# The parts of the turned maxima made on GpSimd instead of VectorE, in a fused attention and mixture-of-experts kernel

## The reference

```python
x = x + 0.5 * _L0_ffn_ref(_layernorm(x), ...)      # 8 experts, the 2 best by a router
x = x + _L0_attn_ref(_layernorm(x), ...)           # 16 heads of 16, causal, 1024 x 1024 scores a head
x = x + 0.5 * _L0_ffn_ref(_layernorm(x), ...)

# in _L0_attn_ref
scores = jnp.einsum('bhqd,bhkd->bhqk', q, k) * (1.0 / np.sqrt(HD))
scores = scores * causal - (1.0 - causal) * NEG
attn = jax.nn.softmax(scores, axis=-1)
out = jnp.einsum('bhqk,bhkd->bhqd', attn, v)
```

## Time and profile before

| | us |
|---|---|
| median of 3 runs | 996.08 (994.55 to 997.16) |
| the profiled execution | 996.42 |
| its span, first to last instruction | 994.7 |
| attention at a steady pace, groups 1 to 13 | 357.06 to 698.25 |
| one slot there | 26.24 |

### The profile page before, as it was taken

The page is one execution under the profiler, slowest core; times in us unless marked ns, Lnnn a source line. Parts: engine busy times, 40 slices in busy tenths (PEclk is TensorE's granted clock), DMA queues, the critical chain, the costliest instruction groups (busy, mean ns, idle before and its releaser), DMA issues.

```text
span 994.7 us, 17662 instructions
## 1 busy us (share of the span) xinstructions
PE 955.4 (96%) x5602; PEld 567.4 (57%) x5602; DVE 830.3 (83%) x2445; ACT 511.0 (51%) x1053; POOL 264.3 (27%) x288
## 2 busy tenths in 40 slices
PE   6899998999998899999999999999998999999998
PEld 4678886777776233333333333333344777777776
DVE  6677777688686899999999999999768788888775
ACT  4235423424315677777777777777775333232310
POOL 1012204202205222222221221222343553434210
PEclk9999999999999899999999999999999999999999
DMA  6201121101023433223222322233320111110001
GB/s 225 90 1 64 51 77 65 37 28 64 34 63 97 128 77 77 78 73 75 61 76 61 72 66 66 72 78 77 92 61 13 43 65 64 64 56 21 8 22 42
DMA packets 55109, 64.32 MB, mean 65 GB/s; under 512 B 13824, under 2 KB 37360, under 8 KB 55024
## 3 DMA queue, kind: packets, MB, share of 16 engines
q1 hardware_dynamic: 54432, 62.47, 22.1%
q10 hardware_dynamic: 592, 0.80, 0.2%
HBM read 41.30 MB, written 21.23 MB: 63 GB/s over the span
## 4 chain that ended last, share of the span: by engine, by line
PE 85%; DVE 7%; issue 3%; ACT 2%; POOL 2%; DMA 1%; DVEq 0%; SPq 0%; ACTq 0%; POOLq 0%
PE bank L362 39%; PE bank L1611 14%; PE bank L1435 13%; PE bank L1593 13%; PE bank L857 2%; PE bank L354 2%; POOL a_part L496 1%; DVE bank L1462 1%; ACT b_probs L1570 1%; DMA v_all<-L_ffn_w_experts 1%; DVE a_acc L1081 1%; PE bank L803 1%; DVE c_acc L1081 1%; POOL b_ks L1408 1%; DVE a_st L317 1%
## 5 line engine op out<-in xcount | busy, mean ns | idle before, releaser
L1570 ACT ACTIVATE b_probs<-bank 128x512 f32<-128x512 f32 (+1 forms) x608 | 302.9, 587 | 114.8 <-PE bank L1593 114.4
L1462 DVE CUSTOM_DVE_ANT_0 bank<-bank,b_below 128x384 f32<-128x384 f32 (+3 forms) x512 | 235.2, 515 | 10.8 <-PE bank L1435 9.3
L1435 PE MATMUL bank<-b_ks,b_qs 96*128 96x512 bf16 (+3 forms) x768 | 222.8, 331 | 10.1 <-DVE b_neg L1462 4.1
L1593 PE MATMUL bank<-b_qs,b_ks 99*128 99x512 bf16 (+3 forms) x768 | 214.9, 331 | 4.5 <-ACT b_probs L1570 4.3
L362 PE MATMUL bank<-we,a_xt 128*128 128x512 f32 x768 | 194.2, 405 | 0.9 <-DVE a_acc L1081 0.9
L362 PE MATMUL bank<-we,c_xt 128*128 128x512 f32 x768 | 186.2, 398 | 0.9 <-DVE c_acc L1081 0.8
L1541 POOL TENSOR_SCALAR_AFFINE_SELECT b_probs<-b_probs 128x512 f32<-128x512 f32 x128 | 83.9, 656 | 323.9 <-ACT b_probs L1570 323.9
L1466 DVE TENSOR_REDUCE b_neg<-bank 128x1 f32<-128x512 f32 x256 | 161.2, 679 | 2.7 <-PE bank L1435 1.2
L362 PEld LDWEIGHTS bank<-we,c_xt 128*128 128x128 f32 x768 | 142.3, 188 | 33.5 <-DVE c_acc L1081 1.9
L362 PEld LDWEIGHTS bank<-we,a_xt 128*128 128x128 f32 x768 | 142.4, 191 | 28.9 <-DVE a_acc L1081 1.5
L1611 PE MATMUL bank<-b_probs,b_vs 128*32 128x512 f32 (+3 forms) x1536 | 156.6, 502 | 0.9 <-POOL b_probs L1541 0.9
(11 more groups left out here) (136 smaller groups left out, 891.1 us busy)
## 6 DMA issues: line engine op xcount, KB each, us to landing
b_qs<-q_parts SPq DMA_DIRECT2D x96, 128.0 KB, 3.0
b_ks<-k_parts SPq DMA_DIRECT2D x96, 128.0 KB, 3.0
q_parts<-a_part SPq DMA_DIRECT2D x16, 384.0 KB, 2.6
k_parts<-a_part SPq DMA_DIRECT2D x16, 384.0 KB, 2.7
att_num<-b_oev SPq DMA_DIRECT2D x64, 64.0 KB, 2.2
c_num<-att_num SPq DMA_DIRECT2D x8, 512.0 KB
c_rec<-att_rec SPq DMA_DIRECT2D x16, 256.0 KB
out<-xs SPq DMA_DIRECT2D x7, 512.0 KB, 3.3
```

Source lines behind the costliest of these rows:

```text
L1435: last = nc.tensor.matmul(ms[bank][:, a * width:(a + 1) * width], qs[g.u][0:ROWS, c, i * P:(i + 1) * P], ks[g.u][0:ROWS, c, lo:lo + width] ...
L1462: last = dve.tensor_tensor_reduce(part, part, below[:, CH - width:CH], -1.0, 3.0e38, ALU.add, ALU.min, dst[:, a, :])
L1570: act.activation(probs[b % 4][:, heads[0]:heads[0] + hp, 0:width], es[exp_bank(g, unit)][:, 0:hp * width].rearrange("p (h w) -> p h w", w= ...
L1593: last = nc.tensor.matmul(es[exp_bank(g, unit)][:, a * width:(a + 1) * width], ks[g.u][:, c, j * P:(j + 1) * P], qs[g.u][:, c, first_q:fir ...
```

## The change

VectorE keeps the copy out of PSUM (GpSimd's part works on the copy in SBUF). The four instructions that split the copy go, for groups 1 to 15, into GpSimd's queue, between its select of block 8 and its select of block 9 of the slot before. They wait for that select (`kept`), for the copy (`mread`) and, from the second use of a buffer on, for its earlier placing (`mplaced`); after them GpSimd waits for the last of them. Group 0's parts stay on VectorE. VectorE's copy now waits for the parts of the group before.

```diff
+    def maxima_parts(engine, g, position):
+
+        t, r, m = turned, turned_rest, mparts[g.u]
+        engine.wait_ge(mread, at(position + 1))
+        if g.turn:
+            engine.wait_ge(mplaced[g.u], at(16 * 3 * g.turn))
+        engine.tensor_copy(m[:, 0, :], t[:]).then_inc(mpart, 1)
+        engine.wait_ge(mpart, at(5 * g.n + 1))
+        engine.tensor_tensor(r[:], t[:], m[:, 0, :], ALU.subtract).then_inc(mpart, 1)
+        engine.wait_ge(mpart, at(5 * g.n + 2))
+        engine.tensor_copy(m[:, 1, :], r[:]).then_inc(mpart, 1)
+        engine.wait_ge(mpart, at(5 * g.n + 3))
+        engine.tensor_tensor(m[:, 2, :], r[:], m[:, 1, :], ALU.subtract).then_inc(mpart, 2)
+
     def max_read(dve, entry, position, bank):
         g, n = entry
         dve.wait_ge(mscore, at(position + 1))
         if n is None:
-            t, r, m = turned, turned_rest, mparts[g.u]
-            dve.tensor_copy(t[:], ms[bank][0:GH * KT, 0:P]).then_inc(mread, 1)
-            dve.wait_ge(mread, at(position + 1))
-            if not (isinstance(g.turn, int) and g.turn == 0):
-                dve.wait_ge(mplaced[g.u], at(16 * 3 * g.turn))
-            dve.tensor_copy(m[:, 0, :], t[:]).then_inc(mpart, 1)
-            dve.wait_ge(mpart, at(5 * g.n + 1))
-            dve.tensor_tensor(r[:], t[:], m[:, 0, :], ALU.subtract).then_inc(mpart, 1)
-            dve.wait_ge(mpart, at(5 * g.n + 2))
-            dve.tensor_copy(m[:, 1, :], r[:]).then_inc(mpart, 1)
-            dve.wait_ge(mpart, at(5 * g.n + 3))
-            dve.tensor_tensor(m[:, 2, :], r[:], m[:, 1, :], ALU.subtract).then_inc(mpart, 2)
+            dve.wait_ge(mpart, at(5 * g.n))
+            dve.tensor_copy(turned[:], ms[bank][0:GH * KT, 0:P]).then_inc(mread, 1)
+            if g.n == 0:
+                maxima_parts(dve, g, position)
             return
...
                     pool.affine_select(out=part, in_=part, compare_op=ALU.is_ge, fill=0.0, base=0,
                                        pattern=[[0, GH], [1, P]], channel_multiplier=-1).then_inc(kept, 1)
+                if b == 8 and exists(g + 1):
+                    pool.wait_ge(kept, at(len(sel_blocks) * g.n + sel_blocks.index(b) + 1))
+                    turn = [n for n, (entry, _, _) in enumerate(placed(g)) if entry[1] is None][0]
+                    maxima_parts(pool, g + 1, placed(g)[turn][1])
+                    pool.wait_ge(mpart, at(5 * (g.n + 1) + 5))
                 if b == 2 and exists(g + 1):
```

## The result

The changed kernel takes **1003.84 us** in the median of 4 runs (1003.48 to 1010.09), the kernel before 995.93 on the same chip: a ratio of 1.0096 [1.0074, 1.0118]. The change makes the kernel slower. 1003.6 us was forecast, and the way it was forecast, a wait in every steady slot for the placed parts, by which the slot grows 0.41 us, is what the trace shows.

A forecast was written before the change was run, and what follows sets the result against it. The prediction took TensorE to set the steady pace, with VectorE a close second. Its terms 5.3 + 0.6 + 0.4 + 1.2 = 7.5 us gave 1003.6 us; the forecast's own bounds were 999 to 1012, the stated range 996 to 1011.

The forecast's parts named there:

- step 1: VectorE loses four instructions in each of 15 groups, freed 1.15 us a slot; TensorE's rate hides it, counted as 0.
- step 2: The parts start behind select 8, which ends at 483.80, no longer behind the copy at 481.0.
- step 3: The four instructions take longer on GpSimd: 1.73 us in sum, ends 1.53 and 2.26.
- X: Time of GpSimd's chain from select 8's end to the last part: 1.73 us forecast; TensorE's wait begins at 1.32.
- step 4: At the next group's first exponential matmul TensorE waits 0.41 us for the placing, in 13 steady slots: 5.3 us.
- step 5: Slot 0 is tighter: its matmul comes at 357.68 against 357.06, 0.6 us.
- step 6: In slot 14 the chain runs beside VectorE's product c_att and is slowed: about 0.4 us, between 0 and 1.
- step 7: Single late issues or landings of placings are no longer hidden: some three events, 1.2 us, from 0 to 1.6.
- step 8: Select 9 with its products and the later loads, queued behind the parts and placings, cost 0.
- the cover holds: Rival: X is under 1.32, parts land before TensorE wants them; 994.7 to 996.5, say 995.8; chance 0.14.
- VectorE was the bound: Rival: TensorE only follows VectorE, so each of 15 groups gives 1.15 us; 17 us, 979; chance 0.05.
- mutual blocking: Rival: GpSimd and VectorE block each other in every slot, TensorE waits 1.51 a slot; 23 us, 1019; chance 0.07.

The follow-up runs named there:

- e1: The changed kernel with GpSimd's chain of four instructions moved ahead of select 8 in slots 0 to 13; 995.18 us, ratio 0.9997.
- e3: The changed kernel with SyncE placing each part as soon as it is there, not all three behind the last; 995.09 us, ratio 0.9997.
- e5: The kernel before with one more VectorE copy of 32 x 128 numbers in every slot; 998.26 us, ratio 1.0039.
- e2: The changed kernel with the first two of the four instructions back on VectorE, the last two on GpSimd behind select 8; 1005.32 us, ratio 1.0099.
- e4: The changed kernel with two more casts of the turned maxima on GpSimd at the head of the chain; 1026.1 us, ratio 1.0301.
- e7: The changed kernel with 43 semaphore increments ahead of VectorE's first instruction; 1009.46 us, ratio 1.0153.
- e8: The changed kernel with 144 semaphore increments ahead of TensorE's first instruction; 1018.76 us, ratio 1.0229.

## Why the prediction was right, point by point

- **What bounds the kernel**: TensorE's starts set the pace, and relief of VectorE is worth almost nothing (step 1). The worth is right: 0.04 us a slot in `e1` and `e3`, though the time freed was overestimated (1.15 us forecast, and from the copy's start to the next masked maximum 0.39 us now instead of 1.40, so 1.01). The order is wrong by a hair: VectorE did not follow TensorE, it set the pace, with 0.04 us a slot more than TensorE needs. It waits for nothing there, and `e5` shows that it had no room. The distances of the earlier trace rows could not tell this, since 0.04 us spread over a slot does not show in them. The forecast did not need it. A change that adds to VectorE would have been misjudged by it.
- **The parts start later** (step 2): select 8 ends at 487.88 and the first part starts at 487.95. Right.
- **The chain** (step 3): X = 1.73 us forecast, 1.76 measured (487.88 to 489.64). The terms: casts 0.28 each, not 0.25; the products of two inputs 0.42 and 0.42, not 0.48 and 0.42; the steps between them 0.07, 0.08, 0.07 and 0.14, so 0.36 together, not 0.33. The two-input shape was overestimated by the line through 256 and 1024 elements, the casts underestimated, and the errors met. By the rule of the Trainium skill (GPSIMD Engine Reference, section 4.1, Engine selection) X would have been an estimated 1.88. Here two inputs took 0.42 against VectorE's 0.28, 1.5 times and not 2, and one input 0.28 against 0.22, 1.3 times.
- **The placing lands later than TensorE wants it** (step 4): 0.41 us forecast, and 26.65 - 26.24 = 0.41 measured; 13 x 0.41 = 5.3 us. The mechanism is right, the last 0.04 us of the agreement is luck: without a late placing the relieved slot is 26.21 (`e1`, `e3`), so the wait itself is 0.45 us, as an X of 1.76 over 1.32 has it, and the relief of step 1, counted as 0, hides the difference. That the wait comes again in every slot, and that it begins at X = 1.32, was tested from both sides: `e2` with 0.91 has no wait, `e4` with 2.45 has 0.70 more than the changed kernel (27.35 - 26.21 = 1.14 in all, and 2.45 - 1.32 = 1.13). `e3` takes the landing forward alone and the loss is gone.
- **Slot 0** (step 5): 0.6 forecast; the bracket at its end is 0.52 (in the steady slots such a bracket is 0.1 less than the growth from start to start), and the parts land 4.91 us behind select 8's end of 354.38. The size is right, but the slot as a whole got shorter (34.90 to 34.12), because its stretch at the lower level was shorter. No step had the clock in it.
- **Slot 14** (step 6): 0.4 forecast, with GpSimd blocked beside VectorE's product. POOL, DVE and PE there:

```profile
730.45 0.28 POOL L1445 CAST b_mparts<-b_turned 32x128 bf16<-32x128 f32 x1 [0.91 <-POOL b_probs L1547]
730.81 1.28 POOL L1447 TENSOR_TENSOR b_turned_rest<-b_turned,b_mparts 32x128 f32<-32x128 f32 x1
732.16 0.28 POOL L1449 CAST b_mparts<-b_turned_rest 32x128 bf16<-32x128 f32 x1
732.59 0.42 POOL L1451 TENSOR_TENSOR b_mparts<-b_turned_rest,b_mparts 32x128 bf16<-32x128 f32 x1 [0.15 <-POOL b_mparts L1449]
```

```profile
730.57 1.24 DVE L1097 TENSOR_TENSOR c_att<-c_num,c_rec 128x1024 f32<-128x1024 f32 x1 [0.25 <-DMA c_rec<-att_rec]
```

```profile
733.98 0.85 PE L1622 MATMUL bank<-b_probs,b_vs 128*32 128x384 f32 x8 [0.34 <-POOL b_probs L1547]
```

  One two-input instruction takes 1.28 us there instead of 0.42, beside VectorE's of 730.57 to 731.81, and TensorE waits 0.34 us for the select behind. Right in kind, place and size. The experiments that keep parts on GpSimd show it too: in every one of them one instruction of 32 x 128 takes 1.15 to 1.35 us beside this product in slot 14, and nowhere else. The Trainium skill (Perfetto Trace Analysis, section Optimizing Scalar/DVE Operations) has the two engines share a read port of SBUF; this row agrees, and the thirteen steady slots, where the same instruction takes 0.42 each time while VectorE works on maxima, show that the block is not there beside all of VectorE's work.
- **Late placings** (step 7): 1.2 us forecast, between 0 and 1.6; three came, landing 0.17, 0.25 and 0.33 us late, 0.75 together (an expectation above has 0.36 for the last). The count and the mechanism (a long issue, a long landing) are right, the size was a little high. In `e4` the same term is 5.1 us more, and `e7` has 2.3: it depends on where the fetches fall, and the upper end of 1.6 would not have held for another layout of the same kernel.
- **What is queued behind** (step 8): 0. In the table of waits TensorE never waits for a select of the steady slots, nor for the loads of queries and keys, which start at 493.53, 27.38 us into the slot and not 26.22. In `e4`, at X = 2.45, the products do wait for select 9 (4.0 us in 11 waits), just past the 2.26 where the forecast put the end of that cover; as it said, this is not paid twice, since the slot grows no more than the chain.

The sum was 7.5 us. The four terms came out at 5.3 + 0.5 + 0.3 + 0.8 = 6.9, and the profiled execution at 1003.48, 7.1 above the one before. The agreement is better than the working deserves: +3.1 us up to slot 0 and some -3 us in slots 0 and 14 are stretches at the lower clock level that changed places, and they happen to cancel. The rivals: *the cover holds* needed X under 1.32 and fell with the four rows; *VectorE was the bound*, with a gain of 1.15 us a slot, fell with `e1`: it did set the pace, but TensorE needs only 0.04 us a slot less; *mutual blocking* in every slot did not happen; it came once, in slot 14.

## What to carry over

Before you move a dependent step to an engine with free time, look at what stands ahead of it in that engine's queue and how long the result's transfer takes until its reader wants it: here 1.76 us of slow chain cost nothing one place earlier in the same queue, 5.3 us behind one select, and nothing again when the transfers were issued part by part. And test an engine's slack by giving it a little work: an idle share of 2%, as VectorE's here, may be only the steps between instructions, and an engine that waits for nothing has no slack.

## What the runs showed of the hardware

- The last of three transfers of 8 KB landed 1.0 to 1.9 us later where a 16 KB instruction fetch started 1.8 to 2.6 us behind the first issue (11 of 11 cases), and the second issue took 0.16 to 0.8 us more where one started beside it (10 of 11). Under the cover of 2.35 us in `e1` delays of up to 0.64 us cost nothing; without a cover each is paid.
- The place of VectorE's instructions alone is worth 6.3 us in the last stage (265 against 271.4, `e2` and `e7` against all others), with two gaps of 2.5 to 2.8 us and 6.8 us at the lower clock level behind them. An edit can thus cost 0.6% at a place where it changes nothing; two of the traces, side by side, tell it from an effect of the edit.
- In `e4` TensorE stood idle for 1.6 to 2.3 us five times for a late placing, and each time the granted clock fell from 1.00 to 0.50 for 3.4 us, 1.0 to 1.9 us after it had gone on. In `e8` it stood 1.76 us once, and in `e2` and `e7` 1.3 to 1.5 us three times, and the clock stayed at 1.00. Since one of the five was only 1.6 us long, the length of the wait alone does not tell them apart; what does was not looked into.
- GpSimd on 32 x 128: a cast 0.28 us, a subtraction of two inputs 0.42, and 0.07 to 0.14 us from one to the next that waits for it. Beside VectorE's product of two SBUF tensors, one of them took 1.15 to 1.35 us.
